# First image of a fused attention kernel: another order of its steps, and the weight-times-bias rows moved from VectorE to GpSimd and ScalarE

## The reference

```
h = group_norm(x); q, k, v = conv1x1(h, wq, bq), conv1x1(h, wk, bk), conv1x1(h, wv, bv)
attn = softmax(einsum('bci,bcj->bij', q, k) * C ** -0.5, axis=2)
out = einsum('bcj,bij->bci', v, attn); out = conv1x1(out, wo, bo)
return x + out
```

## Time and profile before

| | |
|---|---|
| median of three runs | 1980.87 us (1979.98 to 1981.94) |
| the profiled execution | 1980.81 us |
| its span | 1978.8 us |
| PE busy | 1965.7 us, 99% |
| DVE busy | 1632.2 us, 82% |
| ACT busy | 999.0 us, 50% |
| POOL busy | 316.4 us, 16% |
| granted TensorE clock, mean | 0.999 of full |

### The profile page before, as it was taken

The page is one execution under the profiler, slowest core; times in us unless marked ns, Lnnn a source line. Parts: engine busy times, 40 slices in busy tenths (PEclk is TensorE's granted clock), DMA queues, the critical chain, the costliest instruction groups (busy, mean ns, idle before and its releaser), DMA issues.

```text
span 1978.8 us, 29821 instructions
## 1 busy us (share of the span) xinstructions
PE 1965.7 (99%) x9920; PEld 1678.5 (85%) x9920; DVE 1632.2 (82%) x2288; ACT 999.0 (50%) x1526; POOL 316.4 (16%) x239
## 2 busy tenths in 40 slices
PE   9999999999999999999999999999999999999999
PEld 7788888888888888888888888888888888888887
DVE  8898796988969789697887979879698896978857
ACT  6464462645536464454644536446264553646443
POOL 2022120121201112020121201212012120111202
PEclk9999999999999999999999999999999999999999
DMA  7336153362523634145350543615336252363402
GB/s 250 128 149 162 62 160 108 148 170 97 130 91 148 170 148 119 50 165 153 148 159 24 173 132 148 161 65 156 106 148 170 104 126 88 149 169 148 91 32 43
DMA packets 55035, 254.66 MB, mean 129 GB/s; under 512 B 8160, under 2 KB 8160, under 8 KB 50400
## 3 DMA queue, kind: packets, MB, share of 16 engines
q1 hardware_dynamic: 35136, 221.01, 29.5%
q0 software_dynamic: 18288, 33.30, 10.7%
q10 hardware_dynamic: 1584, 0.01, 0.1%
HBM read 213.39 MB, written 74.45 MB: 145 GB/s over the span
## 4 chain that ended last, share of the span: by engine, by line
PE 94%; DVE 0%; issue 0%; POOL 0%; ACT 0%; POOLq 0%
PE psum L426 31%; PE psum L427 31%; PE psum L428 31%; DVE red L1200 0%; DVE scores L1205 0%; POOL wide L401 0%; DVE scores L1191 0%; DVE scores L1390 0%; DVE scores L1259 0%; ACT room L754 0%; POOLq L400 0%; ACT scores L768 0%
## 5 line engine op out<-in xcount | busy, mean ns | idle before, releaser
L426 PE MATMUL psum<-big_hi 128*128 128x512 f32 x1056 | 411.2, 389 | 1.3 <-DVE big_lo L1016 0.7
L427 PE MATMUL psum<-big_lo,big_hi 128*128 128x512 f32 x1056 | 411.0, 389 | 0.0
L428 PE MATMUL psum<-big_hi,big_lo 128*128 128x512 f32 x1056 | 410.8, 389 | 0.0
L426 PE MATMUL psum<-big_hi,h_hi 128*128 128x512 f32 x896 | 349.2, 390 | 3.3 <-DVE scores L1082 3.3
L427 PE MATMUL psum<-big_lo,h_hi 128*128 128x512 f32 x896 | 349.3, 390 | 0.0
L428 PE MATMUL psum<-big_hi,h_lo 128*128 128x512 f32 x896 | 349.1, 390 | 0.0
L1191 DVE TENSOR_TENSOR scores<-psum,room 128x512 f32<-128x512 f32 x192 | 130.7, 689 | 202.3 <-ACT room L849 152.3
L849 ACT COPY room<-psum 128x512 f32<-128x512 f32 x192 | 113.3, 590 | 290.4 <-PE psum L428 290.3
L426 PE MATMUL psum<-w_split,h_hi 128*128 128x256 f32 x896 | 253.6, 283 | 0.5 <-ACT room L754 0.5
L428 PE MATMUL psum<-w_split,h_lo 128*128 128x256 f32 x896 | 253.6, 283 | 0.0
L427 PE MATMUL psum<-w_split,h_hi 128*128 128x256 f32 x896 | 253.5, 283 | 0.0
(11 more groups left out here) (138 smaller groups left out, 3434.9 us busy)
## 6 DMA issues: line engine op xcount, KB each, us to landing
w_split<-kept_t SPq DMA_DIRECT2D x15, 3584.0 KB, 12.2
w_split<-kept_v SPq DMA_DIRECT2D x15, 3584.0 KB, 11.2
room<-in_x SPq DMA_DIRECT2D x64, 512.0 KB, 3.4
out<-scores POOLq DMA_DIRECT2D x127, 256.0 KB, 6.8
room<-in_x SPq DMA_DIRECT2D x61, 256.0 KB, 5.8
red<-in_x SPq DMA_DIRECT2D x30, 256.0 KB, 3.7
wide<-in_x SPq DMA_DIRECT2D x30, 256.0 KB, 6.8
kept_t<-w_split SPq DMA_DIRECT2D x1, 3584.0 KB, 10.9
```

The lines of the kernel that those rows point to most:

```text
L426: nc.tensor.matmul(o, a_hi, b_hi, start=start, stop=False, skip_group_check=True)
L427: nc.tensor.matmul(o, a_hi, b_lo, start=False, stop=False, skip_group_check=True)
L428: return nc.tensor.matmul(o, a_lo, b_hi, start=False, stop=stop, skip_group_check=True)
```

## The change

On ScalarE, VectorE and PE the written-out order of image 0's t stage is changed, and the waits are renumbered to fit. The order of the high parts of h becomes that of the low parts. VectorE makes the sum B21 and the low part of D4 earlier and B22 later. The four `row_dots` leave VectorE: behind its first `prime`, GpSimd multiplies the four chunks of the outputs' weight with the bias, in place, and ScalarE sums each row with the accumulator of an activation. VectorE waits for the first of these sums before it writes D3 over chunk 0, and for all four before it adds `bo`.

```diff
-H_FIRST_HIGH = (A22, A12, S1, S3, A11, S2, S4)
+C_FIRST = ("D3", "D1", "D2", "B11", "B21", "B22")
+L_FIRST = ("D3", "B11", "D4", "D2", "D1", "B22", "B21")
...
# GpSimd, behind prime() and before the loop of the images
             for o in range(1, KC):
                 low_wv(o)
             prime()
+
+            pool.wait_ge(bv_in, 16)
+            pool.wait_ge(wo_turned, KC)
+            for c in range(KC):
+                nc.gpsimd.tensor_tensor(wo_raw[:, c, :], wo_raw[:, c, :], bv_rows, ALU.mult).then_inc(bv_terms_set, 1)
...
# ScalarE
+            def row_sum(c):
+                act.wait_ge(bv_terms_set, c + 1)
+                nc.scalar.activation(wo_raw[:, c, :], wo_raw[:, c, :], ACT.Identity,
+                                     accum_out=wo_bv[:, c:c + 1]).then_inc(bv_used, 1)
             def first_parts():
-                for r in range(2):
-                    snap(0, r, 0, "a", T_FIRST_AT[4], True)
+                snap(0, 0, 0, "a", T_FIRST_AT[4], True)
                 high_h(0, 2, True)
+                snap(0, 1, 0, "a", T_FIRST_AT[4], True)
+                high_h(0, 3, True)
                 copy_wov(0)
                 copy_wov(1)
-                high_h(0, 3, True)
-                high_h(0, 5, True)
                 high_h(0, 4, True)
                 for r in range(2):
                     snap(0, r, 1, "b", T_FIRST_AT[2], True)
+                row_sum(0)
+                high_h(0, 5, True)
+                high_h(0, 6, True)
+                for c in range(1, KC):
+                    row_sum(c)
                 for r in range(2):
                     high_t(0, r, "D3", True)
-                high_h(0, 6, True)
...
# VectorE
-            def row_dots(c):
-                if c:
-                    dve.wait_ge(bv_used, c)
-                nc.vector.tensor_tensor_reduce(out=wo_bv_terms, in0=wo_raw[:, c, :], in1=bv_rows, scale=1.0,
-                                               scalar=0.0, op0=ALU.mult, op1=ALU.add,
-                                               accum_out=wo_bv[:, c:c + 1]).then_inc(bv_used, 1)
             def make_first_t():
                 low_h(0, 2, True)
+                sum_h(0, 2, True)
                 low_h(0, 3, True)
-                sum_h(0, 2, True)
-                dve.wait_ge(bv_in, 16)
-                dve.wait_ge(vec_in, 16)
-                row_dots(0)
+                sum_h(0, 3, True)
                 low_h(0, 4, True)
-                low_h(0, 5, True)
-                row_dots(1)
+                dve.wait_ge(bv_used, 1)
                 dve.wait_ge(wov_summed, KC)
                 add_t(0, 0, "D3", True)
-                sum_h(0, 3, True)
+                low_h(0, 5, True)
                 add_t(0, 1, "D3", True)
-                for c in (2, 3):
-                    row_dots(c)
                 low_h(0, 6, True)
+                dve.wait_ge(vec_in, 16)
                 dve.wait_ge(bv_used, KC)
                 nc.vector.tensor_tensor(out_bias[:], wo_bv[:], bo_s, ALU.add).then_inc(biases_set, 1)
...
                 low_both("D3")
                 add_both("D1", "D2", "B11")
-                low_both("D4", "B11", "D2", "D1")
-                add_both("B22", "B21")
+                low_both("B11")
+                low_t(0, 0, "D4", True)
+                add_t(0, 0, "B21", True)
+                low_t(0, 1, "D4", True)
+                add_t(0, 1, "B21", True)
+                low_both("D2", "D1")
+                add_both("B22")
                 low_both("B22", "B21")
```

More of the change, by code:

```diff
@@ L48 @@
 H_FIRST_AT = {x: n + 1 for n, x in enumerate(H_FIRST)}
-H_FIRST_HIGH = (A22, A12, S1, S3, A11, S2, S4)
-H_FIRST_HIGH_AT = {x: n + 1 for n, x in enumerate(H_FIRST_HIGH)}
 S_ORDER = tuple((7, q) for q in range(4)) + tuple(
@@ L58 @@
 C_AT = {x: n + 1 for n, x in enumerate(C_ORDER)}
+C_FIRST = ("D3", "D1", "D2", "B11", "B21", "B22")
+C_FIRST_AT = {x: n + 1 for n, x in enumerate(C_FIRST)}
 PRODUCT_OF = {"D3": 7, "D1": 5, "D2": 6, "B11": 1, "B22": 3, "D4": 4, "B21": 2}
@@ L61 @@
 L_AT = {PRODUCT_OF[x]: n + 1 for n, x in enumerate(L_ORDER)}
+L_FIRST = ("D3", "B11", "D4", "D2", "D1", "B22", "B21")
+L_FIRST_AT = {PRODUCT_OF[x]: n + 1 for n, x in enumerate(L_FIRST)}
 G_ORDER = ("D3", "D1", "D2", "D4", "B11", "B22", "B21")
@@ L179, in attention_program @@
         wov_d = [scores[:, n, :].rearrange("p (k n) -> p k n", k=2) for n in (10, 11, 14, 15)]
-        bv_rows, wo_bv_terms = scores[:, 13, :], scores[:, 12, :]
+        bv_rows = scores[:, 13, :]
         psum = ctx.enter_context(nc.psum_tensor("psum", [P, 8, 512], F32))
@@ L237, in attention_program @@
             sem(n) for n in ("consts_set", "max_all", "sum_all", "rstd_set", "wv_split", "reduce_begun"))
-        wt_copied = sem("wt_copied")
+        wt_copied, bv_terms_set = sem("wt_copied"), sem("bv_terms_set")
         primed, wv_first = sem("primed"), sem("wv_first")
@@ L496, in make_first_t @@
                         if p == 1:
-                            pe.wait_ge(t_added, t_count(0, True, 6, r, C_AT["D3"]))
+                            pe.wait_ge(t_added, t_count(0, True, 6, r, C_FIRST_AT["D3"]))
                         t_product(0, r, p)
@@ L530, in make_scores @@
                     if q % 2 == 0 or p == 7:
-                        pe.wait_ge(t_split, t_count(b, first, 7, 1, L_AT[p]))
+                        pe.wait_ge(t_split, t_count(b, first, 7, 1, (L_FIRST_AT if first else L_AT)[p]))
                     if p == 7:
@@ L538, in make_scores @@
                         elif q == 2:
-                            pe.wait_ge(t_added, t_count(b, first, 6, 0, C_AT["D1"]))
+                            pe.wait_ge(t_added, t_count(b, first, 6, 0, (C_FIRST_AT if first else C_AT)["D1"]))
                         else:
-                            pe.wait_ge(t_added, t_count(b, first, 6, 0, C_AT["D2"]))
+                            pe.wait_ge(t_added, t_count(b, first, 6, 0, (C_FIRST_AT if first else C_AT)["D2"]))
                     if p == 1:
                         if q == 0:
-                            pe.wait_ge(t_split, t_count(b, first, 7, 0, L_AT[4]))
-                            pe.wait_ge(t_added, t_count(b, first, 6, 0, C_AT["B21"]))
+                            pe.wait_ge(t_split, t_count(b, first, 7, 0, (L_FIRST_AT if first else L_AT)[4]))
+                            pe.wait_ge(t_added, t_count(b, first, 6, 0, (C_FIRST_AT if first else C_AT)["B21"]))
                         elif q == 1:
-                            pe.wait_ge(t_added, t_count(b, first, 6, 1, C_AT["D1"]))
+                            pe.wait_ge(t_added, t_count(b, first, 6, 1, (C_FIRST_AT if first else C_AT)["D1"]))
                         else:
@@ L558, in make_scores @@
                         if q == 0:
-                            pe.wait_ge(t_added, t_count(b, first, 6, 1, C_AT["D2"]))
+                            pe.wait_ge(t_added, t_count(b, first, 6, 1, (C_FIRST_AT if first else C_AT)["D2"]))
                         elif q == 1:
-                            pe.wait_ge(t_split, t_count(b, first, 7, 1, L_AT[4]))
-                            pe.wait_ge(t_added, t_count(b, first, 6, 1, C_AT["B21"]))
+                            pe.wait_ge(t_split, t_count(b, first, 7, 1, (L_FIRST_AT if first else L_AT)[4]))
+                            pe.wait_ge(t_added, t_count(b, first, 6, 1, (C_FIRST_AT if first else C_AT)["B21"]))
                         else:
@@ L746, in high_t @@
                 else:
-                    act.wait_ge(t_added, t_count(b, first, 6, r, C_AT[name]))
+                    act.wait_ge(t_added, t_count(b, first, 6, r, (C_FIRST_AT if first else C_AT)[name]))
                     nc.scalar.copy(t_hi[:, OF_T[p], r, :], t_sum(first, r, name)).then_inc(t_high, 1)
@@ L983, in low_h @@
                 a = (H_FIRST if first else H_ORDER)[n]
-                dve.wait_ge(h_high, H_FIRST_HIGH_AT[a] if first else count(b, 7, n + 1))
+                dve.wait_ge(h_high, H_FIRST_AT[a] if first else count(b, 7, n + 1))
                 if a not in (A11, A12, A22):
@@ L1057, in made @@
                 def made(other):
-                    dve.wait_ge(t_added, t_count(b, first, 6, r, C_AT[other]))
+                    dve.wait_ge(t_added, t_count(b, first, 6, r, (C_FIRST_AT if first else C_AT)[other]))
                     return t_sum(first, r, other)
```

## The result

The changed kernel takes 1991.34 us (median of 6 runs, 1990.60 to 1992.79), against 1981.07 us (6 runs of the kernel before). The ratio is 1.005 with a 95% interval of 1.004 to 1.006: slower by 10.3 us, a tenth of what I had forecast. The profiled execution took 1992.79 us with a span of 1991.1 us, against a span of 1978.8 us. Some 1 us of this difference is the start: a weight's DMA landed later (PE waited 0.7 us for `in_wo`), and everything behind it is that much later in this one execution.

What follows compares the result with a forecast made beforehand. PE, busy 1965.7 of 1978.8 us, was taken to bound the kernel. 1980.8 - 0.7 (t stage) + 7.6 (image 0's switch) + 89.7 (images 1 to 14) = 2077.4 us, range 2045 to 2110.

Steps and rivals of the forecast that it cites:

- The switch stands in the loop's body, in front of L401, behind the wait.: GpSimd's code load before the maximum's all-reduce stands in the loop's body, where nothing hides it; 5.94 us.
- where it runs in all 15 turns, needed or not: GpSimd's switch back to all-reduce code is paid every loop turn, 5.94 us each; chance 0.80.
- the 14 x 6.41 = 89.7 us of the sum: Images 1 to 14 each lose 6.41 us: PE stalls 4.76 us in the values, plus 1.65 of lower clock.
- the 8.29 us ahead of the program's first operation: GpSimd's idle time at L364, with no other code before it, taken as evidence against the chip passing over resident code.
- once only: Rival: the chip passes over a load of code already there, image 0 alone pays; 1987.7 us, chance 0.05.
- The price of one exposed switch: PE's loss per image behind the maximum's all-reduce: 6.41 us in images 1 to 14, 7.6 in image 0.
- the clock's part: Time lost to PE's lower clock level behind an exposed switch: 1.65 us of image 0's 7.6.
- the list behind the sum: Alternative totals: 2051 us without the clock's part, 2092 with 6.91 us a switch, 2112 with 8.29.
- The detour of the row sums is hidden.: Image 0's t stage: GpSimd products at 1.28 us each, ScalarE's last row sum at 45.7 to 46, no delay.
- The t stage gains 0.7 us by the orders.: Image 0: B21's wait goes, a 4.3 us stall on the scores' copy comes; gain 0.7 us, bounds 2.3 and -1.
- My end of product 7: Product 7 of image 0's scores ends 1.4 us earlier, at 57.4.
- The price of the clock.: PE drops to its lower clock level behind stalls longer than 3.28 us, costing 1.65 us each.

Runs made afterwards that it cites:

- experiments 2 and 1: Kernel before plus a small GpSimd tensor_tensor: at the head of every loop turn, 2081.90 us (2); once behind the first prime, 1990.28 us (1).
- experiment 5: The changed kernel's orders with the four row sums left on VectorE, nothing added to GpSimd or ScalarE: 1983.02 us, ratio 1.0005 to the kernel before.
- 3: The changed kernel with a second prime behind GpSimd's four products: 1984.36 us, ratio 1.0014 to the kernel before.
- experiment 8: Changed kernel with second prime behind the products, B22 summed directly behind B11, and values' weight parts each behind a pair of score copies: 1978.32 us.
- experiment 4: The changed kernel with its single prime moved behind GpSimd's four products: 1985.05 us, ratio 1.0015 to the kernel before.

## Why the prediction was wrong

I forecast 2077.4 us (2045 to 2110) and slower; it is slower, by 10.3 us. By the steps of the prediction:

- *The switch stands in the loop's body, in front of L401, behind the wait.* Right: 15 pairs there, and in image 0 the all-reduce begins 6.2 us behind the last maximum.
- *"where it runs in all 15 turns, needed or not"*, at 5.94 us. **This step failed.** It runs in all 15, but where the code is already there it costs 0.15 us, and the 14 x 6.41 = 89.7 us of the sum are not there. I had read the 8.29 us ahead of the program's first operation, with no other code before it in the program, as a load of resident code. The trace doesn't say what was resident at that point, so it could not carry that. My rival "once only", 1987.7 us with a chance of 0.05, was the mechanism that came true. It stands 6.9 us above before and the kernel 10.3: the rest is the t stage, which I had taken for a small gain. That the kernel is slower at all comes from image 0 alone, which both cases share.
- *The price of one exposed switch*, 6.41 us in images 1 to 14 and 7.6 in image 0. Right in size: 6.5 and 8.3 us (experiments 2 and 1). Of the 7.6 the clock's part was too small: behind 119.78 the lower level lasts until 124.42, which is 22 matmuls of 256 columns (by PE's weight loads; 21 matmuls are recorded) in 4.64 us, in place of 22 x 0.12 = 2.64. That is 2.0 us, not 1.65. In the list behind the sum, 8.29 us a switch gives 2112.7 and not 2112.
- *The detour of the row sums is hidden.* Wrong. I took a product for 1.28 us, from a row in which VectorE had no instruction with two inputs from SBUF beside it (until 16.57 it made the statistics of `room`, which have one input), and gave the hindrance 1 to 2 us in total. It is 2.28 us a product, the last sum came at 50.4 in place of 46, and with the low parts of h, which get longer too, it costs 1.3 us against experiment 5 (1984.36 and 1983.02 in the same rounds) and 3.3 us once the later wait is out of the way.
- *The t stage gains 0.7 us by the orders.* Their effect is +1.0 us, within the bound that I gave (a loss of 1), and within what can't be told from none. The mechanism was right, the wait for B21 turned into one on the scores' copy, and the size was off: 5.5 us in place of 4.3 in experiment 5. Two terms were mis-sized. One is the time of the high part of B11: ScalarE had it at 54.8 rather than 53.1, with D1's sums at 50.05, which there stand behind the three row sums that VectorE still makes. The other is the lower clock behind the wait, 2.4 us and not 1.65. My end of product 7 was also 0.4 us too early: 62.31 - 3.28 - 1.26 is 57.8, not 57.4. In the changed kernel itself the wait is 4.15 us, close to my 4.3, but that is luck: PE was ready at 64.87 and not at 60.1, the copy at 68.9 and not at 64.4, both over 4 us late.
- *The price of the clock.* The forecast that PE falls to its lower level behind each long wait was right for the waits of 4.15 and 6.66 us of the changed kernel; it also fell behind the 1.82 us at 52.09, which I had not forecast. As a rule it doesn't hold (last section).

The difference of 10.3 us is made up so: the orders +1.0 (experiment 5, not clear of no change by itself), the moved rows +1.3 (3 against 5), the exposed switch +8 (the changed kernel against 3). It is one way to divide it: with B22 in its better place the moved rows cost 3.3 us.

## What to carry to other kernels

When an engine gets new work, look at what kind of work stands next in its program, and not only at its idle time: here an operation of 1 us behind the last `prime` cost 8.3 us, because the switch back was paid 70 us later, behind a wait where nothing hides it. Restore the old state right behind the new work, while the engine is idle. And price moved work by a row in which its neighbour is as busy as it will be: GpSimd's product and VectorE's low part each take up to nearly twice as long when they meet, so free time on GpSimd is no free time while VectorE is the one that PE waits for.

## What the runs showed that I had not expected

- A load of GpSimd code that is already there is passed over: the all-reduce begins 51.92 us behind its predecessor in place of 51.77. The Trainium skill says (GPSIMD Engine Reference, 2.1 Instruction dispatch) that the first call of freshly loaded code pays about 6 us; the runs agree, with 6.2 us in image 0, and add that the loading instructions alone, without new code, don't.
- GpSimd and VectorE hinder each other both ways, and it hangs on where VectorE reads: two inputs from SBUF, 1.22 to 2.3 us for 128x1024 (and 2.49 to 5.76 us for four of 128x512), one from PSUM, no change (0.74, and 1.28 for two). The Trainium skill (GPSIMD Engine Reference, 1. Specifications) names the contention with VectorE instructions that have two SBUF inputs; the runs agree, with these sizes.
- The rows fit taking turns, and not a shared speed. Read one by one, the four products of the changed kernel start at 40.66, 42.95, 45.17 and 47.41 and take 2.27 to 2.31 us. The VectorE instruction that was there first (40.61) keeps its 1.22 us, and the product ends 1.1 us behind it, at 42.97; the next (41.75) starts during the product and ends 1.1 us behind the product's end. The last product ends at 49.68, though VectorE is idle from 48.54. With some 1.25 us for a product alone and 1.13 for a 128x1024 of VectorE, each waiting for the other's current instruction, all of these lengths come out: the one that starts at 44.71, for instance, ends at 46.30, 1.1 us behind the end of the second product at 45.22. This is read from the traces; no experiment was made for it.
- The clock's fall isn't a matter of the wait's length alone: it fell behind waits of 1.82 and 1.83 us (changed kernel at 52.09, experiment 8 at 51.43) and not behind one of 2.96 us (experiment 4 at 40.66). The wait of 3.28 us on B21 brought it down in the profiled execution of the kernel before (62.31), and the same wait of 3.28 us in experiment 2 (62.49) didn't. What decides it, the runs leave open; so the clock's part of such a wait is no fixed number.
